# Second MLP product from scaled fp16 halves, ScalarE normalisation and regrouped VectorE sums in a sandwich-attention kernel

## What is computed

```python
q, k, v = split(shift_token(x) @ wqkv)
q, k = rotary_xpos(l2norm(q) * qs, l2norm(k) * ksc)
x = x + local_attention(q, k, v) @ wo            # windows of 128 rows
h = shift_token(x)
h = (h - mean(h)) / sqrt(var(h) + 1e-05) * lg + lb
a, g = split(h @ w1 + b1)                        # hidden width 682
x = x + (a * gelu(g)) @ w2 + b2
```

## Time and profile before

| what | us |
|---|---|
| median of 3 runs (3177.8 to 3181.57) | 3178.43 |
| span of the profiled execution, first to last instruction | 3177.2 |
| busy: PE / DVE / ACT / POOL | 2982.5 / 2656.8 / 1847.9 / 1754.4 |

### The profile page before, as it was taken

How to read it: one execution, slowest core, us unless ns; L and a number is a source line. 1 busy time by engine, 2 the same in 40 slices (tenths; PEclk the granted TensorE clock), 3 DMA queues, 4 the chain that set the end, 5 groups by cost and what they waited for, 6 DMA issues and landing times.

```text
span 3177.2 us, 79721 instructions
## 1 busy us (share of the span) xinstructions
PE 2982.5 (94%) x24952; PEld 2581.8 (81%) x24952; DVE 2656.8 (84%) x7754; ACT 1847.9 (58%) x4226; POOL 1754.4 (55%) x2083
## 2 busy tenths in 40 slices
PE   6898989783899999999999999999999999999997
PEld 3676767573688888888888888888888888888886
DVE  6878788755788888888888888899998999999895
ACT  4233241402566666666666666666676676676673
POOL 1231314024566666666666666676676676676773
PEclk9999999995899999999999999999999999999999
DMA  1120202025111111111111111222112212122221
GB/s 38 38 70 28 80 14 87 4 83 205 33 50 49 53 51 49 52 48 49 54 50 50 50 48 50 56 56 60 56 55 57 65 55 60 55 55 60 63 56 46
DMA packets 273326, 177.65 MB, mean 56 GB/s; under 512 B 95758, under 2 KB 271090, under 8 KB 272754
## 3 DMA queue, kind: packets, MB, share of 16 engines
q1 hardware_dynamic: 273138, 175.50, 19.0%
HBM read 104.08 MB, written 54.54 MB: 50 GB/s over the span
## 4 chain that ended last, share of the span: by engine, by line
PE 72%; POOL 1%; issue 1%; DVE 0%; DMA 0%; ACT 0%; POOLq 0%; SPq 0%; DVEq 0%; ACTq 0%
PE b_ps L824 17%; PE b_ps L899 14%; PE b_ps L910 10%; PE b_ps L852 8%; PE b_ps L840 7%; PE b_ps L878 6%; PE b_ps L865 6%; PE b_ps L809 2%; PE b_ps L802 2%; PE b_ps L791 1%; POOL b_sq L1145 0%; POOL b_rn L1178 0%; POOL b_t L1167 0%; POOL b_kr L1183 0%; DVE b_probs L1093 0%
## 5 line engine op out<-in xcount | busy, mean ns | idle before, releaser
L957 ACT ACTIVATE b_probs<-b_probs,b_negmax 128x256 f32<-128x256 f32 x1024 | 506.0, 496 | 78.3 <-DVE b_negmax L1093 77.5
L824 PE MATMUL b_ps<-b_wqkv,b_hT_hi 128*128 128x512 f32 x1536 | 493.0, 402 | 1.0 <-DVE b_hT_lo L981 1.0
L899 PE MATMUL b_ps<-b_h2T,b_w 128*128 128x256 f16 x4224 | 473.0, 273 | 6.5 <-DMA b_h2T<-b_xh_hl 6.4
L899 PEld LDWEIGHTS b_ps<-b_h2T,b_w 128*128 128x128 f16 x4224 | 413.6, 98 | 55.1 <-DMA b_h2T<-b_xh_hl 6.8
L1145 POOL TENSOR_TENSOR b_sq<-b_sq 128x512 f32<-128x512 f32 (+5 forms) x768 | 419.3, 546 | 62.4 <-ACT b_sq L938 22.3
L1178 POOL TENSOR_TENSOR b_rn<-b_ss_min,b_mhalf 128x16 f32<-128x16 f32 x128 | 377.2, 2947 | 108.9 <-DVE b_ss_min L1005 108.7
L1106 DVE TENSOR_SCALAR b_probs<-b_probs,b_rinv 128x256 f32<-128x256 f32 x1024 | 409.6, 442 | 18.2
L1155 POOL TENSOR_TENSOR b_rstd<-b_var,b_mhalf 128x1 f32<-128x1 f32 x128 | 72.2, 564 | 552.3 <-DVE b_var L1066 552.3
L407 PE MATMUL a_ps<-a_xn_hl,a_E 128*128 128x256 f16 x3072 | 352.5, 277 | 18.9 <-DVE a_E L290 18.9
L407 PEld LDWEIGHTS a_ps<-a_xn_hl,a_E 128*128 128x128 f16 x3072 | 303.3, 99 | 58.5 <-issue 19.9
L910 PE MATMUL b_ps<-b_w,b_hid 128*128 128x256 f32 x1536 | 342.2, 379 | 1.2 <-DVE b_hid L1129 1.2
(11 more groups left out here) (137 smaller groups left out, 6191.6 us busy)
## 6 DMA issues: line engine op xcount, KB each, us to landing
b_hx<-xs_dram SPq DMA_DIRECT2D x256, 64.0 KB, 1.9
b_rot<-rot_dram SPq DMA_DIRECT2D x128, 128.0 KB, 2.1
b_xr<-xs_dram SPq DMA_DIRECT2D x128, 128.0 KB, 2.1
xp_dram<-b_xp SPq DMA_DIRECT2D x128, 128.0 KB, 1.7
b_h<-xp_dram SPq DMA_DIRECT2D x256, 64.0 KB, 1.8
a_x_res<-in_L_attn_x_dram SPq DMA_DIRECT2D x64, 128.0 KB, 2.2
x_dram<-a_x SPq DMA_DIRECT2D x64, 128.0 KB, 1.7
xs_dram<-a_xo SPq DMA_DIRECT2D x64, 128.0 KB, 1.8
```

Of the source, the lines that this page charges most:

```text
L824: last = nc.tensor.matmul(ps[:, bank, :], hT[:, k, :], wqkv[:, ds(layer(s), 1), part, k, bank * INNER:(bank + 1) * INNER], start=(k == 0 a ...
L899: last = nc.tensor.matmul(ps[:, bank, half * 2 * P:(half + 1) * 2 * P], w1[:, ds(layer(2 * j), 1), wp, k, first:first + P], h2T[:, hp, k, ...
L957: nc.scalar.activation(probs[:, h, :], probs[:, h, :], ACT.Exp, bias=negmax[:, h:h + 1], scale=-1.0, accum_out=rowsum[:, h:h + 1]).then_in ...
```

## The change

1. The second MLP product: `w2` and `hid` are kept as two fp16 halves each, scaled by powers of two. PE makes three fp16 products (high x high, high x low, low x high) in place of each fp32 one. The halves of `hid` are made by POOL: per pair six copies to fp16 and six subtractions, four chunks at the end of its even slot and two in its odd slot behind `rstd2`. PE waits for the last of them (`hid_lo`). The scale is taken out again in `xpp`.
2. Normalisation of the MLP's input: DVE no longer makes `xh` and its fp16 copy. DVE makes the negated mean, POOL the product `shift2 = -mean * rstd2`, and ACT two `Identity` activations with scale and bias: `xh` between the squares of q and k, the fp16 copy between the square of k and the copy of v.
3. The statistics move to a function `norm_stats`: in odd slots it stands where it did, in even slots it is the first thing that DVE does.
4. DVE's rotation takes two products in place of three; POOL does one halving in place of six, and DVE sums the rest in one reduction `sum_squares` right after the rotation of k; the powers of k's and q's norms are two instructions of 8 in place of one of 16; four reciprocals of two heads become two of four.
5. The preparation: `w2` and `b1` are loaded ahead of the rotation tables, a bound for `hid` is computed with a second reduction over partitions, and `w2` is split into its halves.

```diff
 PE, odd slot
-                        pe.wait_ge(hid_ready, HC * (j + 1))
+                        pe.wait_ge(hid_lo, HC * (j + 1))
...
-                                last = nc.tensor.matmul(ps[:, 3, n * D:(n + 1) * D], hid[:, c, n * P:(n + 1) * P], w2[:, ds(layer(2 * j), 1), c, :],
-                                                        start=(c == 0), stop=(c == HC - 1))
+                                for a, (hp, wp) in enumerate(PARTS):
+                                    last = nc.tensor.matmul(ps[:, 3, n * D:(n + 1) * D], hid_hl[:, hp, c, n * P:(n + 1) * P],
+                                                            w2[:, ds(layer(2 * j), 1), wp, c, :],
+                                                            start=(c == 0 and a == 0), stop=(c == HC - 1 and a == 2))
 ACT
                         nc.scalar.activation(sq[:, 0:HEADS, :], by_head(ps[:, 0, :]), ACT.Square).then_inc(q_sq, 1)
+                        act.wait_ge(shift2_ready, t + 1)
+                        wait(act, xh_lo, t)
+                        nc.scalar.activation(xh[:], h2[:, (r - 3) % 2, :], ACT.Identity, bias=shift2[:], scale=rstd2[:]).then_inc(xh_ready, 1)
                         nc.scalar.activation(sq[:, HEADS:2 * HEADS, :], by_head(ps[:, 1, :]), ACT.Square).then_inc(k_sq, 1)
+                        wait(act, h2T_loaded, 16 * t)
+                        nc.scalar.activation(xh_hl[:, 0, :], h2[:, (r - 3) % 2, :], ACT.Identity, bias=shift2[:], scale=rstd2[:]).then_inc(xh_hi, 1)
 DVE
+                def sum_squares(s):
+                    if in_range(s):
+                        dve.wait_ge(ss_halved, s + 1)
+                        wait(dve, ss_ready, s)
+                        nc.vector.tensor_reduce(ss[:], sq[:, :, 0:DH // 2], AX.X, ALU.add).then_inc(ss_summed, 1)
+
+                def norm_stats(s, r):
+                    t = s - 3
+                    if in_range(t):
+                        dve.wait_ge(h2_loaded, 32 * (t + 1))
+                        nc.vector.bn_stats(st2[:], h2[:, (r - 3) % 2, :]).then_inc(st2_ready, 1)
+                        wait(dve, shift2_ready, t)
+                        wait_apart(dve, st2_ready, t + 1, passed_dve)
+                        nc.vector.bn_aggr(mv2[:], st2[:]).then_inc(mv2_ready, 1)
+                        dve.wait_ge(mv2_ready, t + 1)
+                        nc.vector.tensor_scalar(var2[:], mv2[:, 1:2], EPS, None, ALU.add).then_inc(var2_ready, 1)
+                        nc.vector.tensor_scalar(negmean2[:], mv2[:, 0:1], -1.0, None, ALU.mult).then_inc(negmean2_ready, 1)
...
                 def run(s, r, pairs, layer):
+                    if r % 2 == 0:
+                        norm_stats(s, r)
...
                                                 ALU.subtract).then_inc(kT_lo, 1)
+                    if r % 2 == 1:
+                        norm_stats(s, r)
                     layer_output(pairs - 3, r, layer)
...
                     rotate(s, r, 1, k_sq, k_terms, kr_ready)
+                    sum_squares(s)
                     output_stats(pairs - 3, r, layer)
 POOL
+                def hid_halves(j, first, end):
+                    if in_range(2 * j):
+                        wait(pool, w2_done, j)
+                        for c in range(first, end):
+                            rows = slice(0, P if c < FULL else REST)
+                            wait_apart(pool, hid_ready, HC * j + c + 1, passed_pool)
+                            nc.gpsimd.tensor_copy(hid_hl[rows, 0, c, :], hid[rows, c, :]).then_inc(hid_hi, 1)
+                            pool.wait_ge(hid_hi, HC * j + c + 1)
+                            nc.gpsimd.tensor_tensor(hid_hl[rows, 1, c, :], hid[rows, c, :], hid_hl[rows, 0, c, :], ALU.subtract).then_inc(hid_lo, 1)
...
                         nc.gpsimd.tensor_tensor(rstd2[:], var2[:], mhalf[:, 0:1], ALU.pow).then_inc(rstd2_ready, 1)
+                        pool.wait_ge(negmean2_ready, t + 1)
+                        pool.wait_ge(rstd2_ready, t + 1)
+                        nc.gpsimd.tensor_tensor(shift2[:], negmean2[:], rstd2[:], ALU.mult).then_inc(shift2_ready, 1)
+                    if r % 2 == 1:
+                        hid_halves(pairs - 2, HID_EARLY, HC)
+                    if in_range(s):
+                        pool.wait_ge(k_sq, s + 1)
+                        nc.gpsimd.tensor_tensor(sq[:, :, 0:DH // 2], sq[:, :, 0:DH // 2], sq[:, :, DH // 2:DH], ALU.add).then_inc(ss_halved, 1)
...
+                    if r % 2 == 0:
+                        hid_halves(pairs - 2, 0, HID_EARLY)
```

More of the change, by code:

```diff
@@ L42 @@
 SECOND_REST = P // 2
+A_COLUMNS = FULL * P + SECOND_REST
 assert 0 < REST <= P // 2
@@ L49 @@
 W1_TOP = 2.0 ** 13
+W2_TOP = 2.0 ** 13
+HID_TOP = 2.0 ** 14
+ROW_BOUND = 272.25
 NT = LAYERS * NW
@@ L621, in _ @@
+                dve.wait_ge(scale_ready, 1)
+                nc.vector.reciprocal(w1a_unit[:], w1a_scale[:]).then_inc(step, 1)
+                dve.wait_ge(step, 13)
+                nc.vector.tensor_tensor(w2_unit[:], w1a_unit[:], w2_low[:], ALU.mult)
                 for l in range(LAYERS):
@@ L998, in rotate, with factor @@
-                        nc.vector.tensor_tensor(t2_h[:, :, half:DH], x[:, :, 0:half], factor(2 * n + 1, half, DH), ALU.mult).then_inc(terms, 1)
+                        by_half = lambda ap: ap.rearrange("p (h c d) -> p h c d", c=2, d=DH // 2)
+                        def factor(which):
+                            return rot[:, r % 2, which:which + 1, :].to_broadcast([P, HEADS, DH])
+                        nc.vector.tensor_tensor(by_head(t1[:, n, :]), by_head(ps[:, n, :]), factor(2 * n), ALU.mult).then_inc(terms, 1)
@@ L1124, in run @@
                     if r % 2 == 0 and in_range(2 * j):
-                        wait(dve, w2_done, j)
+                        wait(dve, hid_lo, HC * j)
                         for c, bank in enumerate(W1_BANKS):
@@ L1136, in _ @@
             def _(pool):
-                def halve(s, first, end):
-                    if in_range(s):
-                        pool.wait_ge(k_sq, s + 1)
-                        for n in range(first, end):
-                            width = DH >> (n + 1)
-                            target = sq[:, :, 0:width]
-                            wait(pool, ss_halved, HALVINGS * s + n)
-                            nc.gpsimd.tensor_tensor(target, target, sq[:, :, width:2 * width], ALU.add).then_inc(ss_halved, 1)
+                def hid_halves(j, first, end):
[7 more added lines that the diff above has]
+                            nc.gpsimd.tensor_tensor(hid_hl[rows, 1, c, :], hid[rows, c, :], hid_hl[rows, 0, c, :], ALU.subtract).then_inc(hid_lo, 1)
                 def run(s, r, pairs, layer):
```

207 lines of the change are left out of this document (116 added, 91 removed).

## The result

The changed kernel is slower: the ratio to the kernel before is 1.0298, with a 95% interval of 1.0279 to 1.0317. Its profiled execution took 3275.35 us (span 3273.6), a second one 3272.23, beside 3178.79 for the kernel before in the same session. Two further executions, of 6009 and 10622 us, are left out as disturbed. Forecast were 3260 us and a range of 3185 to 3345.

A forecast was written before the change was run, and what follows sets the result against it. PE, gapless, was taken to bound the loop. Saving less stalls gave +0.70 us per pair in layer 0 and +1.70 in layer 1, 77 over 32 pairs each; with +5 for preparation, 3260 us, range 3185 to 3345.

The forecast's parts named there:

- PE's saving: Second MLP product on PE: 36 fp16 matmuls take 3.93 us instead of 5.18, saving 1.25 per pair.
- Even slots: DVE's statistics wait for h2's load, delaying qT's low part and PE's v projection: stall 1.5 us per pair, 1.7 in layer 1.
- Odd slots: ACT taking over xh delays the copies of probabilities and PE's product with v: stall 0.45 us per pair.
- what comes off DVE: xh, its copy, two reciprocals and two rotation starts per slot leave DVE, off PE's path in the loop: gain nothing.
- Odd slots of layer 1: POOL's late halving delays DVE's sum of squares and oT's low part, holding the output projection by 0.8 us.
- POOL at the end of even slots: Four hid chunks of 1.32 us end just as rstd2 is due: cost nothing, without margin.
- rival of a late POOL: Slower chunks of 1.7 us make rstd2 and xh 1.5 later in each odd slot: 3356 us, chance 0.13.
- Preparation and first slots: DVE gains 9 us of preparation work; the halved power for k returns 4 over three slots: net +5 us.
- only the v stall bites: Rival: ACT and POOL have slack, leaving the v projection's stall, 1.4 against 1.25 saved per pair: 3193 us, chance 0.17.

The follow-up runs named there:

- e9: Changed kernel with DVE and ACT queues reordered, one-column variance, w2/b1 loads later, and even-slot xh and its half behind the probability copies: 3139.9 us, ratio 0.9872.
- e11: Changed kernel with even-slot statistics still first on DVE but read from xp in SBUF, not h2; ACT's xh waits for h2: 3190.5 us, ratio 1.0034.
- e5: Changed kernel with the output variance plus EPS written as two 128x1 tensor_scalar instructions instead of one 128x2: 3241.3 us, ratio 1.0187.
- e2: Changed kernel with the sum of squares moved behind layer 1's output statistics in DVE's queue: 3289.4 us, ratio 1.0346.
- e1: Changed kernel with even-slot statistics put back behind the low parts of qT and kT in DVE's queue: 3254.9 us, ratio 1.0236.
- e3: Changed kernel with ACT squaring k before it writes xh: 3260.3 us, ratio 1.0250.
- e6: Changed kernel with the edits of e2, e3 and e5, and even-slot statistics behind the low part of qT and behind xpp: 3169.9 us, ratio 0.9964.

## Why the prediction was right, and where not

The direction and the main cause were right. That the size came so near, 3260 against 3272 to 3275, is in part luck. Per pair the prediction set 1.95 us of stalls in layer 0 and 2.95 in layer 1 against 1.25 saved; the windows have 1.44 and 2.47 us of idle PE against 0.61 and 0.55 saved. Over the loop the stalls were thus taken 32 us too large and the saving 43 too large; with 3 us too little for the preparation that leaves the 14 us between forecast and measurement. Point by point:

- **PE's saving**, 1.25 a pair: 1.23 in the product itself, right. But PE's busy time fell by only 34.7 us in all (2982.5 to 2947.8) and not by the product's 78.8. Of the other 44 us, 17 are in the projections and 9 in the product with v, which ran slower; neither was in the sum. The remaining 18 are not accounted for. In e9, with most of the stalls gone, PE is busy for 2922.0, 60 us less than before.
- **Even slots**, 1.5 a pair by the landing of `h2`: the trace has the chain step by step and e11 shows that the landing and not the work is at fault. The size was 1.3 (80.6 us over 62 even slots), not 1.5 and 1.7.
- **Odd slots**, 0.45 by ACT: 0.16, and 0.15 more because the product runs at the pace of the copies. Two errors met. `xh` and its half hold ACT for about 0.5 each (`xh` starts at 1382.24, the next instruction at 1382.75), not 0.25: here 256 elements from SBUF cost as much as 512 from PSUM. But `shift2` came 2.5 us ahead of the product's turn and not 1.8, since DVE began the low part of qT 1.4 behind PE's q transposes instead of 2.0; its products `hid` ahead of that had begun 0.9 earlier against them. The prediction put what comes off DVE at nothing; these 0.6 us were not in it. Which of the things taken off DVE bought them no run shows.
- **Odd slots of layer 1**, 0.8 by the sum of squares: 0.9, for another reason. This is the step that failed: "POOL ends the halving ... the low part of oT starts at 1355.15, 1.0 late". The 1.26 us of output statistics were taken over from the earlier trace rows as if their price did not depend on what POOL does beside them. They cost 2.41, because the addition of two columns among them is held until POOL's run ends. With that gone (e5) the late halving costs nothing; with the halving's wait taken out and the two-column form left (e2) it gets worse.
- **POOL at the end of even slots**, no cost: right, with more margin than thought. A copy took 0.40, a chunk 1.09 and not 1.32, and `rstd2` in odd slots waits for DVE, not behind the halves:

```profile
1362.43 0.40 POOL L1214 CAST b_hid_hl<-b_hid 128x256 f16<-128x256 f32 x1
1362.91 0.68 POOL L1216 TENSOR_TENSOR b_hid_hl<-b_hid,b_hid_hl 128x256 f16<-128x256 f32 x1
1364.13 0.56 POOL L1227 TENSOR_TENSOR b_rstd<-b_var,b_mhalf 128x1 f32<-128x1 f32 x1 [0.54 <-DVE b_var L1084]
```

  The rival of a late POOL is out. ACT loads its tables 126 times before and after; that agrees with what the Trainium skill (ScalarE: Activation LUTs, section on table sets) says of identity, that it is in every set.
- **Preparation and first slots**, +5: +8. The preparation alone is 13 longer (774.38 to 787.64). Its eleven early loads were not costed: they push POOL's first rotation product 7.6 back (741.21 against 733.58). While it runs DVE is held, here in a product of a single column with both inputs in SBUF, which ends 0.02 behind POOL's; in the kernel before POOL's product fell on two scalings, which took 7.36 us there (the like pair ahead of it 1.82). So this wait of DVE is not new, it moved back with POOL's product:

```profile
742.02 8.02 DVE L627 TENSOR_TENSOR p_top_sq<-p_top 128x1 f32<-128x1 f32 x1
```

  and in the kernel before:

```profile
736.65 7.36 DVE L607 TENSOR_SCALAR p_w_f<-p_w_f,p_lg 128x1408 f32<-128x1408 f32 x2 [4.38 <-PE b_ps L580]
```

The rival "only the v stall bites" missed that three stalls stood one behind the other: e1 takes the v stall away and gets 20 of 81 us. (Its 1.4 a pair is not the 1.5 that the chain had worked out; with 1.5 it would have said 3199.)

## What to carry to other kernels

A wait for a transfer belongs as far back in an in-order queue as its consumers allow, and all that stands behind it, on that engine and on those it feeds, has to be asked what it makes wait: removing one such stall shows the next, so the edits are worth most together (by the ratios e1, e2, e3 and e5 gave 20, -15, 15 and 35 us alone, and 106 in e6, where `xpp` was moved ahead as well). When work goes to GpSimd, look at every VectorE instruction from SBUF to SBUF that will run beside it, even one of two numbers a row: it may end only when GpSimd's run does.

## What was not expected of the hardware

- A VectorE `tensor_scalar` of 128x2 took 0.17 to 4.04 us, the long ones ending with POOL's run; of 128x1, 0.14 to 0.16 in all 64 of e5. A `tensor_tensor` of 128x1 with both inputs in SBUF took 8.02 beside a POOL product of 8.81.
- POOL's instructions that follow one another without a gap let the 128x2 form through only behind the last: 4.04 us spanned the halving, the low half of `xh` and both sums. A gap of 0.08 between two POOL instructions was enough in the kernel before.
- ScalarE's `Identity` with scale and bias on 128x256 in SBUF takes 0.60 us, a square of 128x512 in PSUM 0.57 to 0.60.
- The fp32 projections' matmuls went from 389 to 395 ns (median) with the clock granted in full in both; cause open.
